# Two attention layers on one core: pairs of PSUM banks for the row maxima, and a new table of when each job runs

## The reference

```python
x = x + _L0_conv_ref(_gn(x), ...)    # global attention, 1024 keys, bias from two relative tables
x = x + _L1_conv_ref(_gn(x), ...)    # each query sees a 7x7 neighbourhood and 16 registers
```

```python
scores = q @ swapaxes(k) * SCALE + attn_bias         # layer 0, 1024 x 1024 for each head
attn = softmax(scores, axis=-1)                      # layer 1: where(mask, scores, -1e30) first
out = (attn @ v) @ w_proj.T + b_proj
```

## Time and profile before

| | us |
|---|---|
| median of 3 runs | 4869.68 |
| the 3 runs | 4855.43 to 4874.59 |
| the profiled execution | 4862.39 |
| its span | 4860.6 |
| one turn of the loop, 1750.40 to 2041.10 in it | 290.7 |
| of it L0 main, 1883.9 to 2041.1 | 157.2 |
| of it L1 main, 1778.6 to 1853.4 | 74.8 |
| TensorE busy, share of the span | 91% |
| VectorE busy | 63% |
| ScalarE busy | 53% |

### The profile page before, as it was taken

One profiled execution on the slowest core, in us unless ns is written; L12 is line 12 of the kernel. 1 busy time (PEld: TensorE's weight loads), 2 busy tenths in 40 slices (PEclk: granted clock), 3 DMA queues, 4 the chain that ended last, 5 costly groups with the idle time before them and its releaser, 6 DMA issues.

```text
span 4860.6 us, 97545 instructions
## 1 busy us (share of the span) xinstructions
PE 4446.6 (91%) x32598; PEld 2268.6 (47%) x32598; DVE 3079.8 (63%) x5558; ACT 2594.1 (53%) x3955; POOL 892.4 (18%) x1901
## 2 busy tenths in 40 slices
PE   4879999999999999999999999999999999999988
PEld 3334453544535454453544535454453544535434
DVE  3736667666675756657566675756757566675644
ACT  1533556555564655555555565555546555565564
POOL 4122021222202222021222202222031221202111
PEclk7988999999999999999999999999999999999999
DMA  6333152442514433153442424433253432424402
GB/s 123 87 73 77 44 119 64 100 87 56 107 42 107 88 89 75 44 115 68 100 80 58 101 52 103 91 83 75 45 114 75 100 80 49 103 60 100 88 15 40
DMA packets 235869, 386.05 MB, mean 79 GB/s; under 512 B 58396, under 2 KB 133728, under 8 KB 235360
## 3 DMA queue, kind: packets, MB, share of 16 engines
q1 hardware_dynamic: 189280, 266.13, 23.7%
q10 hardware_dynamic: 21504, 75.51, 7.8%
q0 software_dynamic: 24576, 37.80, 4.9%
HBM read 227.79 MB, written 88.08 MB: 65 GB/s over the span
## 4 chain that ended last, share of the span: by engine, by line
PE 71%; DVE 11%; issue 6%; DMA 5%; SPq 5%; ACT 2%; DVEq 0%; ACTq 0%; POOL 0%
PE P L1143 14%; PE P L1161 13%; PE P L1102 12%; DVE mx L909 7%; PE P L966 5%; PE P L967 5%; PE P L1193 4%; PE P L1214 4%; DMA queries<-oraw 4%; PE P L1110 3%; PE P L1079 3%; SPq L514 3%; DVE mxc L915 2%; PE P L1186 1%; PE P L1231 1%
## 5 line engine op out<-in xcount | busy, mean ns | idle before, releaser
L909 DVE TENSOR_REDUCE mx<-P 128x1 f32<-128x512 f32 x3072 | 1921.3, 684 | 457.4 <-PE P L1102 453.3
L779 ACT ACTIVATE probs<-P 128x1024 f32<-128x1024 f32 x1536 | 1507.5, 1022 | 854.0 <-PE P L1161 853.8
L1102 PE MATMUL P<-K,AR 96*128 96x256 f16 x6144 | 1074.1, 278 | 56.6 <-DMA AR<-biases 29.5
L1161 PE MATMUL P<-AR,K 113*128 113x512 f16 x3072 | 924.9, 383 | 13.2 <-DMA AR<-mrow 12.6
L915 DVE TENSOR_REDUCE mxc<-P 128x1 f32<-128x336 f32 (+1 forms) x1536 | 656.3, 474 | 317.9 <-PE P L1111 315.0
L1143 PE MATMUL P<-probs,V 128*17 128x512 f32 x6144 | 813.5, 601 | 5.7 <-ACT probs L779 5.7
L1102 PEld LDWEIGHTS P<-K,AR 96*128 96x128 f16 x6144 | 532.2, 98 | 581.4 <-DVE mx L909 202.0
L795 ACT ACTIVATE probs<-P 128x320 f32<-128x320 f32 (+3 forms) x1632 | 612.1, 437 | 338.2 <-PE P L1214 268.4
L1161 PEld LDWEIGHTS P<-AR,K 113*128 113x128 f16 x3072 | 213.3, 98 | 670.3 <-ACT probs L779 519.6
L1110 PE MATMUL P<-K,A 112*128 112x320 f16 (+1 forms) x1536 | 405.2, 300 | 68.7 <-DVE mx L909 54.9
L1214 PE MATMUL P<-A,K 113*128 113x320 f16 (+2 forms) x1536 | 428.3, 300 | 14.7 <-ACT probs L795 14.3
(11 more groups left out here) (125 smaller groups left out, 3718.4 us busy)
## 6 DMA issues: line engine op xcount, KB each, us to landing
AR<-biases SPq DMA_DIRECT2D x384, 256.0 KB, 7.9
AR<-queries ACTq DMA_DIRECT2D x96, 512.0 KB, 5.9
biases<-xn SPq DMA_DIRECT2D x128, 256.0 KB, 2.6
AR<-queries ACTq DMA_DIRECT2D x96, 256.0 KB, 8.8
K<-oraw POOLq DMA_DIRECT2D x384, 64.0 KB, 4.7
xin<-in_x_dram SPq DMA_DIRECT2D x16, 768.0 KB, 10.5
queries<-oraw SPq DMA_DIRECT2D x384, 32.0 KB, 4.6
QA<-queries SPq DMA_DIRECT2D x192, 64.0 KB, 2.8
```

What stands on the lines that cost most here:

```text
L779: nc.scalar.activation(probs[:, u % RING, j:j + 2, :], P[:, b:b + 2, :], ACT.Exp).then_inc(p_done[0], 1)
L909: V_.reduce_max(mx[:, n // 2, n % 2:n % 2 + 1], bank, AX.X).then_inc(used, 1)
L1102: last = mm(bank[:, QD * (v % 2):QD * (v % 2) + QD], AR[0:ROWS_MAX[0], part % SLOTS, v, c, j, 128 * q:128 * q + 128], K0[0:ROWS_MAX[0], h, ...
L1161: last = mm(P[:, j, :], K0[0:ROWS, h, 128 * kt:128 * kt + 128], AR[0:ROWS, p % SLOTS, kt // 2, :, j, :], start=True, stop=True)
```

## The change

**Banks.** In L0 the scores now rotate over the three banks 0, 1 and 2 one by one, with a wait for the exponential of three scores before, and each of the four scores of a unit has an exponential of 512 columns of its own. The values move to bank 7, and jobs have banks 3 to 6. L1 keeps its banks.

**Pairs.** A job of kind "max2" computes two tiles into two neighbouring banks, and one reduction takes both: 1024 columns to one maximum in L0 (its tiles 2n and 2n+1 hold the two halves of one row's keys), and in L1 two tiles of equal width (`TILE_PAIRS`) to two maxima. It is used in L0 main only; the jobs of L1 main and of the stages before and after the loop stay single. The small reduction ahead of the row is left only for single tiles.

**Rows.** The row is put behind up to two later jobs (`rows_later`), where these lie within two steps and are neither rows nor maxima of layer 1 while the row is of layer 1. Rows have semaphores of their own, and the collected maxima of L0 two buffers, by the parity of the part.

**Table.** Part 1 of the next image leaves its last 12 tiles and its row to the L0 main of that image (`SECOND = 20`): L0 main now has 140 tiles of L0 in 70 pairs, 80 of L1 in 40 pairs, and 7 rows; L1 main has 52 and 16 single tiles and 2 rows. Parts 3, 4 and 5 have 15 steps each instead of 18, 16 and 16, and no stretch mixes them with the jobs of layer 1.

```diff
-SCORES, JOBS = (4, 3), 3
-JOB_BANKS = ((4, 5, 7), (3, 4, 5))
+SCORES = 3
+JOB_BANKS, VALUES_BANK = ((3, 4, 5, 6), (3, 4, 5)), 7
+SINGLES = 2 * STEPS[0]
+TILE_PAIRS = ((0, 7), (1, 2), (3, 4), (5, 6))
-THIRD = 16
+SECOND, THIRD = 20, 16
...
+def max_pairs(layer, image, part):
+    return [("max2", layer, image, part, n) for n in range(0, ITEMS[layer] + 1, 2)]
...
-    return {"rel": 4, "stat": 1, "max": (7, 5)[job[1]]}[job[0]]
+    return {"rel": 4, "stat": 1, "max": (7, 5)[job[1]], "max2": (12, 9)[job[1]]}[job[0]]
...
+def rows_later(placed):
+    for at in [n for n, (_, job) in enumerate(placed) if is_row(job)][::-1]:
+        to, passed = at, 0
+        while passed < 2 and to + 1 < len(placed):
+            place, follower = placed[to + 1]
+            same_layer = follower[0] in ("max", "max2") and follower[1] == placed[at][1][1] == 1
+            if place > placed[at][0] + 2 or is_row(follower) or same_layer:
+                break
+            to, passed = to + 1, passed + (follower[0] not in MOVES)
+        row = placed.pop(at)
+        placed.insert(to, (placed[to - 1][0] if to > at else row[0], row[1]))
+    return placed
...
+        wide = 1 + (job[0] == "max2" and job[4] < ITEMS[job[1]])
+        at += at % wide
+        taken = [ring[(at + k) % len(ring)] for k in range(wide)]
+        before = max((held[b] for b in taken if b in held), default=None)
...
 def plan_l0(image, i1, n0):
     if is_image(image, 0):
-        placed = evenly(max_jobs(0, image, 1), 0, 13) + evenly(max_jobs(0, image, 2), 13, 28)
+        placed = evenly(max_pairs(0, image, 1), 0, 14) + evenly(max_pairs(0, image, 2), 14, 28)
     else:
-        placed = evenly(max_jobs(0, image, 2), 0, 20)
-    placed += evenly(max_jobs(0, image, 3), 27, 45) + evenly(max_jobs(0, image, 4), 45, 61)
-    placed += evenly(max_jobs(0, image, 5), 61, 77)
-    placed += [(8 + 3 * n, job) for n, job in enumerate(rel_jobs(image, 2))]
+        placed = evenly(max_pairs(0, image, 1)[SECOND // 2:] + max_pairs(0, image, 2), 0, 18)
+    for p in (3, 4, 5):
+        placed += evenly(max_pairs(0, image, p), 15 * p - 16, 15 * p)
+    placed += [(18 + 3 * n, job) for n, job in enumerate(rel_jobs(image, 2))]
...
-        placed += evenly(max_jobs(1, i1, 0), 13, 32)
-        placed += evenly(max_jobs(1, i1, 1) + max_jobs(1, i1, 2)[:THIRD], 73, 95)
+        placed += evenly(max_pairs(1, i1, 0), 18, 30)
+        placed += evenly(max_pairs(1, i1, 1) + max_pairs(1, i1, 2)[:THIRD // 2], 75, 95)
...
-    placed += evenly(max_jobs(0, n0, 0) + max_jobs(0, n0, 1), 25, STEPS[1] - TAIL)
+    placed += evenly(max_jobs(0, n0, 0) + max_jobs(0, n0, 1)[:SECOND], 25, STEPS[1] - TAIL)
...
-                        act.wait_ge(st_done[0], im * STEPS[0] + step + 1)
-                        b = 2 * (step % 2)
-                        nc.scalar.activation(probs[:, u % RING, j:j + 2, :], P[:, b:b + 2, :],
-                                             ACT.Exp).then_inc(p_done[0], 1)
+                        for k in range(2):
+                            single = 2 * step + k
+                            act.wait_ge(st_done[0], im * SINGLES + single + 1)
+                            nc.scalar.activation(probs[:, u % RING, j + k, :], P[:, single % SCORES, :],
+                                                 ACT.Exp).then_inc(p_done[0], 1)
...
+                        elif what == "max2" and layer == 0:
+                            V_.reduce_max(mxc[0][:, part % 2, n // 2:n // 2 + 1], banks(at, 2), AX.X).then_inc(used, 2)
...
                         for j in (2 * k, 2 * k + 1):
+                            h, single = GH * (p // 2) + j, 4 * u + j
+                            if single >= SCORES:
+                                pe.wait_ge(p_done[0], im * SINGLES + single - SCORES + 1)
```

More of the change, by code:

```diff
@@ L115, in evenly, with is_row, plan @@
     return placed
[L118 to L121 removed]
+def is_row(job):
+    return job[0] in ("max", "max2") and job[4] == ITEMS[job[1]]
+def rows_later(placed):
[10 more added lines that the diff above has]
+    return placed
+def plan(steps, placed, ring):
+    after, jobs, held, at = [[] for _ in range(steps)], [], {}, 0
+    for place, job in rows_later(sorted(placed, key=lambda p: p[0])):
         if job[0] in MOVES:
@@ L1090, in run_job @@
                     pe.wait_ge(k_in[1][part], (image + 1) * PER_K)
+                tiles = [n + k for k in range(2 if what == "max2" else 1)]
                 if n == ITEMS[layer]:
-                    if layer == 0:
-                        pe.wait_ge(comb_done, image * PHASES[0] + part + 1)
-                        last = nc.tensor.transpose(bank[0:ITEMS[0] // 2, 0:128], mxc[0][:], ident[:])
+                    if layer == 0 and what == "max2":
+                        pe.wait_ge(*consumed(job[:4] + (n - 2,)))
+                        last = nc.tensor.transpose(bank[0:ITEMS[0] // 2, 0:128], mxc[0][:, part % 2, :], ident[:])
+                    elif layer == 0:
+                        pe.wait_ge(comb_done, part + 1 if is_image(image, 0) else image * 2 + part)
+                        last = nc.tensor.transpose(bank[0:ITEMS[0] // 2, 0:128], mxc[0][:, part % 2, :], ident[:])
@@ L1114, in run_jobs @@
+                if is_row(job):
+                    last.then_inc(row_done[layer], 1)
+                else:
+                    last.then_inc(smax_done[layer], len(tiles))
             def run_jobs(entries, L):
```

119 lines of the change are left out of this document (65 added, 54 removed).

## The result

| | before | after |
|---|---|---|
| median | 4866.85 us (4 runs) | **4930.24 us** (4 runs, 4925.94 to 4936.52) |
| ratio, 95% interval | | 1.0134 (1.0115 to 1.0153) |
| span of the profiled execution | 4860.6 | 4926.6 |
| first L0 output of the program, at | 288.7 | 311.3 |
| part of a turn with L1 main (L0 output to L1 output), median | 104.2 | 98.3 |

The change makes the kernel 1.3% slower, where 3.2% faster was forecast. The prediction's range (4640 to 4855) misses it. The 66 us between the two spans are 22.6 us at the start and 13 turns of 3.4 us (44). The part with L0 main holds, beside it, the L1 output and a projection of 30.6 us; so L0 main takes about 167.8 us where 153.2 was forecast. The part with L1 main came out as forecast: 5.9 less a turn, against 6.0. (Kernels that have the same L1 main differ by 2 us in that part, as TensorE's granted clock differs there; see "Open".)

What follows compares the result with a forecast made beforehand. TensorE's program, waits included, was taken as the bound. L0 main 4.0 and L1 main 6.0 us less over 14 turns (140), 13 at the start and 4 in the last L0 main gave 4712 us, range 4640 to 4855.

Steps and rivals of the forecast that it cites:

- VectorE's reduction of a pair: L0 main: reductions of 1.22 us starting every 1.16; only eight three-pair units wait, 0.3 each, 2.4 us.
- Jobs of one bank in a ring of pairs: L0 main: waits of 4 x 1.15 = 4.6 us behind rel jobs and 1 for rows; none listed for stat jobs.
- The 1.15 us of the earlier trace: L0 main before: how long TensorE was read to stand after one rel job, with two single jobs past it.
- Rows: L0 main: rows have two jobs ahead of them, except where the next jobs are of their own layer: 1 us.
- The second rival: Whole kernel: the wait moves with the work, L0 main's waits stay at 19.3; 4865 us, no change; chance 0.13.
- The plain unit: L0 main: a unit of two pairs needs 2.74 us with no wait, against 2.92 with 0.19 of wait before.
- The score ring: L0 main: small unevenness of the single scores, 0.04 us a unit, 1.9 in all.
- third rival: L0 main: fourth score waits for the first's exponential, margin 0.07 us, wait 0.35 a unit; 4978 us; chance 0.11.
- The table: L0 main: plain work grows by 2.9 us, since 12 tiles and a row move in from L1 main.
- The start: Before the loop and image 0's L0 main: 9 us saved by 12 fewer tiles and no row, plus about 4: 13.
- ScalarE was not the bound: L0 main: four half exponentials add 0.26 us a unit on ScalarE, which has 2.74 for it; costed at nothing.
- The slower case: Whole kernel: slower than before by more than 24 us, about 0.5%; chance 0.11.

Runs made afterwards that it cites:

- e3: The changed kernel with single tiles, each with its own reduction, in the four job banks instead of pairs; 4742.49 us, ratio 0.9753.
- e11: e3 with its tiles aligned as pairs would be, so a job of one bank leaves the bank beside it unused; 4865.09 us, ratio 1.0011.
- e1: The changed kernel with each row back right behind the last pair of its part; 4902.51 us, ratio 1.0070.
- e5: The kernel before with only its scores changed: three score banks with half exponentials, three job banks kept; 4970.09 us, ratio 1.0211.
- e4: The kernel before with only the banks changed: three score banks with half exponentials, four job banks with single tiles; 4828.40 us, ratio 0.9928.
- e6: The kernel before, its banks and row positions kept, with the new table and the 12 tiles moved; 4961.65 us, ratio 1.0207.
- e16: The changed kernel with the asks and fills of parts 3 to 5 four to five steps later; 4922.54 us, ratio 1.0117.
- e9: e3 with other places: 16 steps each for parts 3 to 5, layer 1 jobs shifted, image 0 as before; 4882.91 us, ratio 1.0044.
- e14: e9 with the asks and fills of parts 3 to 5 four to five steps later; 4768.50 us, ratio 0.9800.
- e10: The changed kernel with two reductions of one bank each per pair, the wait still for both banks; 4948.64 us, ratio 1.0170.

## Why the prediction was wrong

- **"VectorE's reduction of a pair"** was mis-sized, and it is the step that decided. The duration was right (1220 ns, starts every 1.14 in a run). From it I worked out waits of 0.3 us in eight units, 2.4 a turn (the table has six such units in the first nine, not eight), as if a ring of two pairs had to wait for nothing but VectorE's pitch. The third pair of a unit waits for the reduction of the first, which begins only when both its tiles are there: 3.96 us for the unit, not 3.48, while VectorE idles. Single tiles in the same four banks (e3) take 12.1 us a turn less over units 2 to 47, and bring L0 main to 153.7.
- **Jobs of one bank in a ring of pairs** were under-priced: 4.6 for the rel jobs, 1 for the rows, nothing for the stat jobs. e11 shows that the slots by themselves cost. In the table of units: 27.9 us for the five with rel jobs where the forecast's own terms give 24.0, and 7.9 for the two with stat jobs, where they give 6.7. In a turn with a granted clock of 1.00 the five units with rel jobs take 25.1, so the rel jobs' own term was off by about 1; the larger part there is the clock, for which I had no term.
- **The 1.15 us of the earlier trace rows**, from which I made the 4.6, is the idle time of the weight loads. The matmuls stood for 0.66 there, as the row below shows; the 4.6 came near all the same, by luck.
- **Rows.** I gave all rows a cost of 1 us, since two jobs stood between. In the ring of pairs a row, or the pair behind it, stands for a slot (1.68 and 1.28 us in the rows above), and moving them lost 28 us (e1). The second rival said that waits move with the work; this one moved with the row.
- **The plain unit.** I counted 0.19 of its 2.92 us as a wait that the change would take away. It took 0.09, and the other 0.09 was no wait: 2.83, not 2.74, in a unit that occurs sixteen times a turn.
- **The score ring**, 1.9 us a turn: it costs 5.4 in L0 main's part by e5. In a plain unit the margin of 0.07 us of the third rival held and the fourth score's matmul waits for nothing. In units with narrow jobs less work lies ahead of it: unit 10, with three tiles of layer 1, went from 2.38 to 2.65, in e4 and e5 alike. The rival's price (0.35 a unit) was too high.
- **The table.** I took 2.9 us for the twelve tiles and nothing for where the places lie. By e6 the new places alone cost about 100 us on the old ring.
- **The start**: 13 us of gain became 22.6 of loss. I had no term for the transfers that the moved row is issued with; e16 puts 13 us on them. The rest was not taken apart.
- **Right**: L1 main 5.9 less, to within the 2 us by which that part varies. L0 main's number is reached once the pairs are gone (153.7 in e3), but by another sum, with more for the score ring and the plain units and less for tiles and rows: that is luck. ScalarE was not the bound. Four half exponentials took 2.06 us, against 1.94 for two whole ones: 0.12 a unit, not my 0.26. The Trainium skill ("VectorE: DVE Perf Modes", "The TRN2 errata") gives 172 cycles of fixed cost for each, by which I had estimated 0.28; in a run of four more than half of that is not seen here.

The matmul behind the rel job of the earlier trace rows, in the kernel before:

```profile
1909.12 0.81 PE L1102 MATMUL P<-K,AR 96*128 96x256 f16 x4 [0.66 <-DVE xn L896]
```

The slower case had 0.11, all of it on the score ring. What made the kernel slower was another mechanism, in the same rows that I read for the cost of one rel job: two jobs go past it in a ring of three, and in a ring of two slots one.

**Open**: what makes TensorE's granted clock differ between kernels. It explains that the part with L1 main is about 2 us longer in e3, e4 and e5, which change nothing in it against the changed kernel or the kernel before (100.1 against 98.3, and 106.3 and 106.1 against 104.2): over 13 turns of that part the mean granted clock was 0.94 to 0.95 in these three, and 0.97 in the other two. Of the start, 9.6 us stay open; e6, the new table alone on the old banks, has its first L0 output at 308.9 too, so the table is part of it. And the pairing's 4.8 us a turn are not split between waiting for both banks and the coarser places.

## What to carry to other kernels

Count a ring of buffers in slots, and count every job that passes through it, the smallest too: two wide slots that rel, row and stat jobs also use were worth 188 us less here than the same banks as four narrow ones (e3), though the reduction became shorter. A wait in a ring is a delay inside a unit, and isn't bounded by the busy share of the engine that frees it. A job that is moved away from its wait takes a slot where it goes to; try such a move in the ring for which it is meant, since its sign can change with it. And where a small transfer has a deadline, look at what large transfers are issued at the same time.

## What the runs showed that I had not expected

- Four pieces of 4 KB on SyncE's queue landed 8.8 us after the first issue with 0.75 MB of queries asked for on ScalarE's queue 1.4 us behind them and 1 MB of biases 2.6 us behind; without the queries, 4.1 us (e9 and e14).
- A reduction of 1024 columns takes 1.22 us and frees its two banks together; two of 512 in its place (e10) gained nothing over the whole kernel.
- TensorE's granted clock fell for a moment behind the rel job above, where the engine had stood 1.68 us and 0.29 more: 0.55 in the mean of 3.5 us, so near the lower of its two levels (1.2 and 2.4 GHz), and 1.00 on both sides. Eight matmuls of values took 1.70 us there instead of 1.05. At 0.55 these 3.5 us hold the work of 1.9, so about 1.6 us there are clock and not waits, an estimate; e3's units 9 to 13 show 1.00 in eleven of thirteen turns. The window of the changed kernel:

```profile
1958.30:1961.80 3.50, 3.50 (x19) 1.10 (x18) 1.20 (x3) 1.81 (x4) 0.00 (x0) 0.55 0.11 22
```

and the values among them:

```profile
1958.36 1.70 PE L1203 MATMUL P<-probs,V 128*17 128x512 f32 x8
```

Over L0 main the lower clock takes 2.2 us a turn in the changed kernel and 0.3 in e3; in the part with L1 main it is the other way round (0.97 against 0.94). Over the whole kernel the two have the same mean granted clock (0.964 and 0.962 in the profiled executions), so that the 188 us are waits in the balance and not clock.
